# Silu straight from the front's sums, quad 3's input split by columns, and a new order of all steps in a one-core scan kernel

## The chip, the cores and the metric

The kernel runs on one core of a Trainium2 chip, as one launch. The metric is the device time of one execution in microseconds (us), median of several. A core has five engines with queues of their own: PE (matmul), DVE (vector), ACT (activations and copies), POOL (elementwise here) and SP, whose queue only starts DMAs. Each engine runs its own instructions in the order in which they are written; between engines there are only semaphores. SBUF is the working memory, PSUM the eight banks of 128 partitions x 512 f32 that PE writes. POOL here reads and writes SBUF only.

## The reference, cut to what matters

The input is (8, 96, 64, 64) f32, seen as 8 batches of 4096 tokens with 96 channels. Layer 0 is a group norm, a selective-scan block with layer norm, and a residual. Layer 1 is an attention that is linear (no softmax), folded into one 97 x 97 matrix per batch, and a feed-forward part with rounding to 8-bit floats.

```python
xz = u @ in_proj_w.T                                   # 96 -> 2 x 192
xm, z = xz[..., :192], xz[..., 192:]
xm = silu(causal_conv4(xm) + conv_b)                   # the "u" of the kernel
dt, Bm, Cm = split(xm @ x_proj_w.T, [6, 22])           # 6, 16 and 16 columns
delta = softplus(dt @ dt_proj_w.T + dt_proj_b)
h = exp(delta * A) * h + delta * Bm * xm               # per channel and state: 192 x 16 chains of 4096
y = (sum over states of h * Cm + xm * D) * silu(z)
x = x + layernorm(y @ out_proj_w.T)
t = t + linear_attention(layernorm(t)); t = t + quantized_ffn(layernorm(t))
```

## The kernel before, in words

**Tiles.** The tokens are cut into 64 chunks of T = 512 (8 to a batch). The 192 x 16 recurrences of a chunk fill 24 tiles of 128 partitions x 512, in 6 quads of 4: quads 0 to 3 hold channels 0 to 127, quads 4 and 5 the other 64. For every tile (quad `s`, place `q`) there are a decay on ACT (`decay`, L837: DA = exp(A x delta), into one of two PSUM banks), a scan on DVE (`scan`, L1210: R = DA x R + D along time) and, for each quad, a product with C on POOL (`product`, L663), which PE sums over states into bank Y (`sum_states`, L1523 and L1527). As there are two DA banks, decay j waits for scan j-2, and scan j waits for decay j.

**The inputs D.** D = (delta x u) x B is made quad by quad into three buffers (quad s uses buffer s mod 3). Quads 0 and 1 are made by DVE (L1192), which reads B from a PSUM bank PB that ACT fills just before (`put_b`, L823). Quads 2, 4 and 5 are made by POOL (L642). Of quad 3 DVE makes tiles 0 and 1 (128 x 1024, L1192) and POOL tiles 2 and 3 (128 x 1024, `rest`, L651). The first writer of a buffer waits until the quad that held it is scanned: `rest` and DVE's part of quad 3 wait for quad 0, POOL's quad 4 for quad 1, quad 5 for quad 2.

**The front** (of chunk g+2 in iteration g) is PE's: the convolution over four taps in two parts (512 columns for channels 0 to 127, L1480; 256 for the others, L1483) and the two parts of z (L1446). ACT copies these four sums from PSUM into `raw` in SBUF (`front_evac`, L776 and L780), three of them in iteration g and the last in g+1, and in iteration g+1 takes Silu of `raw` into u and z, 128 x 768 each (`silu`, L786 and L792). Silu and Exp/Ln are in different tables, so a table load of 1283 ns stands before and behind each such pair. Then follow the projection of u (L1498, L1500), its evacuation `state_rows` (L800), `dt_proj`, `parts` (L809), `softplus` (L813), `delta` on DVE (L1220) and delta x u on POOL (`du`, L635). SP writes delta, du and B/C rows to DRAM and reads them back spread over partitions (`ds`, `us`, `Bs`, `Cs`).

**The order** is written out by hand, one function `iteration(g)` for each engine: steps of chunk g (scans), of g+1 and g+2 (front), of g-1 and g-2 (out projection, layer norm, tokens) and of g-10 to g-12 (feed-forward: `norm_x2` L1296, `result` L1301, `up`, `hidden`, `down`). The chunks g-10 and later exist only from iteration 10 on. The two additions of the change's title are `add_x` (L1241, residual of layer 0) and `result` (L1301, residual of the feed-forward), both on DVE.

**PSUM.** Banks G0 to G3 pass from one short use to the next within an iteration. PE waits for the last reader of a bank by calls `freed(progress, k, n)` ahead of the new writer.

Of the kernel before, what the change touches and what calls it, by code (L numbers as in the profile page):

```python
# [9 lines left out]
T = 512  # L10
CH = L // T
HALO = TAPS - 1
S = T + 1
LOW = 128
# [29 lines left out]

BY_DVE = {0: 1, 1: 2, 3: 3}
BY_POOL = {2: 1, 3: 2, 4: 3, 5: 4}
OURS = {3: 2}
# [10 lines left out]
def build(nc, I, cols, out):  # L58
# [7 lines left out]
    with ctx:  # L66
# [135 lines left out]
        raw = sb("raw", [LOW, 2, W2])  # L202
# [69 lines left out]
        front_ev = Progress("front_ev", 4)  # L272
        silued = Progress("silued", 2)
# [24 lines left out]
        by_act = [normed, gset, gn_mean, gn_dev, gn_act, front_ev, silued, st_done, sp_done, b_put, exp_done, post_act,  # L298
# [316 lines left out]
        def _(pool):  # L615
            credit(nc.gpsimd, by_pool)

            def first_delta_u():

                pool.wait_ge(dl_low, 1)  # L620
                pool.wait_ge(silued.sem, silued.at(0, 1))
# [4 lines left out]
            def delta_u(k):  # L626
# [5 lines left out]
                pool.wait_ge(silued.sem, silued.at(k, 1))  # L632
# [12 lines left out]
            def rest(k, s):  # L645
                n = OURS[s]
# [4 lines left out]
                nc.gpsimd.tensor_tensor(D[:, s % NDBU, n:QUAD, :], us[:, n:QUAD, :],  # L651
                                        Bs[:, h, w, :].unsqueeze(1).to_broadcast([128, QUAD - n, T]),
# [43 lines left out]
        def _(act):  # L696
# [70 lines left out]
            def front_evac(k, n, src):  # L767
                evac(k, n, src, n + 1)

            def evac(k, n, src, after):  # L770
                act.wait_ge(front_mm.sem, front_mm.at(k, after))
                if n == 0:
                    act.wait_ge(silued.sem, silued.at(k - 1, 1 if k == 1 else None))
                if n in (0, 3):
                    v = n // 3
                    nc.scalar.activation(raw[:, 0, part(v)], src[:, 0:T - H * v], ACT.Identity,  # L776
                                         bias=cb[:, v:v + 1]).then_inc(front_ev.sem, 1)
                else:
                    v = n - 1
                    nc.scalar.copy(raw[:, 1, part(v)], src[:, 0:T - H * v]).then_inc(front_ev.sem, 1)  # L780
# [1196 lines left out]
```

## Time and profile before

| | us |
|---|---|
| median of 3 runs (2616.61 to 2617.24) | 2617.11 |
| the profiled execution | 2615.23 |
| its span, first to last instruction | 2613.3 |
| DVE busy (97% of the span) | 2538.6 |
| POOL busy (92%) | 2411.7 |
| ACT busy (91%) | 2379.0 |
| PE busy (82%) | 2132.9 |

The granted TensorE clock is 0.934 of full speed on average. Busy time of an instruction runs from its start to its end, and neighbours on one engine overlap a little, so what one more instruction costs its engine is the distance between starts where they stand back to back; the timeline shows it.

### The profile page before, as it was taken

The page shows a single profiled execution, that of the slowest core. Times are in us where ns is not written, and L with a number is a line of the kernel's source. Part 1 is how long each engine was busy: PE and PEld are TensorE (multiplying, and loading weights), DVE is VectorE, ACT ScalarE, POOL GpSimd, SP SyncE. Part 2 cuts the span into 40 slices and gives each one's busy share as a digit, 9 for nine tenths or more (in the row PEclk, how much of TensorE's full clock was granted, in tenths as well). Part 3 has the DMA queues.
Part 4 walks back from the last instruction along what each step waited for, and adds up shares of the span by engine and source line. Part 5 has one row for each costly group of instructions (what it writes and reads, how often), then busy time and mean ns, then how long its engine had stood idle before and what let it go on. Part 6 is the DMA issues. An engine that isn't in the chain of part 4 may idle for free.

```text
span 2613.3 us, 34371 instructions
## 1 busy us (share of the span) xinstructions
PE 2132.9 (82%) x9844; PEld 774.2 (30%) x9844; DVE 2538.6 (97%) x2503; ACT 2379.0 (91%) x3971; POOL 2411.7 (92%) x718
## 2 busy tenths in 40 slices
PE   6677777888888888888888888888888888888878
PEld 3222223323323323323323323323323323323323
DVE  6999999999999999999999999999999999999996
ACT  5777778999999999999999999999999999999977
POOL 4999999999999999999999999999999999999981
PEclk8888888899999999999999999999999999999979
DMA  6455555655656656555656565565566565556533
GB/s 249 165 188 165 175 178 168 201 190 189 212 190 192 207 191 203 195 196 194 199 200 197 192 202 196 192 203 195 191 207 199 184 202 192 186 197 200 171 124 88
DMA packets 171161, 494.43 MB, mean 189 GB/s; under 512 B 23040, under 2 KB 44672, under 8 KB 154144
## 3 DMA queue, kind: packets, MB, share of 16 engines
q1 hardware_dynamic: 170976, 492.25, 56.8%
q8 instruction: 81, 1.33, 0.2%
q14 instruction: 104, 0.85, 0.1%
HBM read 400.28 MB, written 91.88 MB: 188 GB/s over the span
## 4 chain that ended last, share of the span: by engine, by line
DVE 48%; issue 23%; ACT 16%; POOL 8%; PE 4%; DMA 1%; SPq 0%; DVEq 0%; ACTq 0%; POOLq 0%
DVE R L1210 32%; DVE D L1192 8%; ACT DA L837 5%; POOL R L663 3%; POOL D L642 3%; DVE yv L1231 2%; ACT dl L809 2%; DVE xq L1241 1%; ACT un L764 1%; ACT rs L848 1%; ACT PB L823 1%; DVE th L1249 1%; DVE xt L1301 1%; DVE q L1296 1%; ACT fsq L886 1%
## 5 line engine op out<-in xcount | busy, mean ns | idle before, releaser
L1210 DVE TENSOR_TENSOR_SCAN R<-DA,R,D 128x512 f32<-128x512 f32 x1344 | 1642.4, 1265 | 21.4 <-ACT DA L837 19.9
L663 POOL TENSOR_TENSOR R<-R,Cs 128x2048 f32<-128x2048 f32 x383 | 1456.0, 3817 | 103.8 <-DVE R L1210 103.3
L837 ACT ACTIVATE DA<-ds,kept_w 128x512 f32<-128x512 f32 x1536 | 1044.3, 686 | 158.3 <-DVE R L1210 145.5
L642 POOL TENSOR_TENSOR D<-us,Bs 128x2048 f32<-128x2048 f32 x193 | 736.7, 3817 | 8.5 <-DMA us<-lo_d 8.1
L1192 DVE TENSOR_TENSOR D<-us,PB 128x2048 f32<-128x2048 f32 x191 | 363.2, 1901 | 5.7 <-ACT PB L823 5.7
L1523 PE MATMUL Y<-R,kept_w 128*32 128x512 f32 x2048 | 289.6, 659 | 9.0 <-POOL R L663 8.9
L1480 PE MATMUL G<-un,wcv 96*128 96x512 f32 x512 | 261.5, 658 | 20.6 <-ACT rs L848 10.6
L1210 DVE TENSOR_TENSOR_SCAN R<-DA,D 128x512 f32<-128x512 f32 x192 | 222.4, 1204 | 8.7 <-ACT DA L837 8.7
L1446 PE MATMUL G<-sq,kept_w 96*96 96x512 f32 (+1 forms) x256 | 145.5, 651 | 78.0 <-ACT h L900 46.7
L1527 PE MATMUL Y<-R,kept_w 128*32 128x256 f32 x2048 | 158.3, 434 | 5.5 <-POOL R L663 5.5
L1446 PE MATMUL G<-st,kept_w 128*64 128x256 f32 (+1 forms) x384 | 112.5, 485 | 57.4 <-ACT st L800 57.4
L1480 PEld LDWEIGHTS G<-un,wcv 96*128 96x128 f32 x512 | 100.9, 207 | 181.1 <-issue 111.6
L1446 PE MATMUL G<-q,w1q 96*128 96x512 fp8e5 x164 | 67.1, 410 | 105.3 <-ACT rs L848 74.1
L1483 PE MATMUL G<-un,wcv 96*64 96x256 f32 x1024 | 149.4, 416 | 0.0
L651 POOL TENSOR_TENSOR D<-us,Bs 128x1024 f32<-128x1024 f32 x64 | 128.0, 2000 | 0.0
L1537 PE MATMUL Y<-u,kept_w 64*64 64x256 f32 x256 | 49.6, 470 | 91.0 <-DVE yv L1231 90.9
L904 ACT ACTIVATE h<-h,b1q 128x512 f16<-128x512 f16 x165 | 112.0, 711 | 0.0
L1446 PE MATMUL G<-un,kept_w 96*128 96x512 f32 x372 | 110.3, 485 | 0.2
L823 ACT COPY PB<-Bs 128x512 f32<-128x512 f32 x191 | 110.2, 577 | 0.0
L1523 PEld LDWEIGHTS Y<-R,kept_w 128*32 128x32 f32 x2048 | 48.9, 117 | 192.9 <-issue 124.6
L1483 PEld LDWEIGHTS G<-un,wcv 96*64 96x64 f32 x1024 | 65.0, 141 | 128.9 <-issue 110.1
L1498 PE MATMUL G<-u,kept_w 128*128 128x512 f32 x128 | 71.7, 642 | 36.7 <-ACT u L786 36.7
(224 smaller groups left out, 3323.5 us busy)
## 6 DMA issues: line engine op xcount, KB each, us to landing
Bs<-bc_d SPq DMA_DIRECT2D x128, 512.0 KB, 5.2
us<-lo_d SPq DMA_DIRECT2D x64, 1024.0 KB, 6.6
ds<-lo_d SPq DMA_DIRECT2D x64, 1024.0 KB, 6.5
Cs<-bc_d SPq DMA_DIRECT2D x128, 512.0 KB, 4.8
us<-hi_d SPq DMA_DIRECT2D x64, 512.0 KB, 7.2
ds<-hi_d SPq DMA_DIRECT2D x64, 512.0 KB, 4.6
lo_d<-dl SPq DMA_DIRECT2D x64, 256.0 KB, 2.0
lo_d<-du SPq DMA_DIRECT2D x64, 256.0 KB, 2.0
```

The source lines that it names most:

```text
L642: nc.gpsimd.tensor_tensor(shaped(D[:, s % NDBU, :, :], s), low(us, s) if s in LOWS else high(us), of_states(Bs, s), ALU.mult).then_inc(don ...
L651: nc.gpsimd.tensor_tensor(D[:, s % NDBU, n:QUAD, :], us[:, n:QUAD, :], Bs[:, h, w, :].unsqueeze(1).to_broadcast([128, QUAD - n, T]), ALU.m ...
L663: nc.gpsimd.tensor_tensor(shaped(R[:, s, :, 0:T], s), shaped(R[:, s, :, 1:S], s), of_states(Cs, s), ALU.mult).then_inc(hc_done.sem, 1)
L823: nc.scalar.copy(PB[:, :], Bs[:, h, w, :]).then_inc(b_put.sem, steps_to(k, s))
L837: nc.scalar.activation(DA[j % NDA][:, :], ds[:, i, :], ACT.Exp, scale=A[:, j:j + 1]).then_inc(exp_done.sem, 1)
L1192: nc.vector.tensor_tensor(D[:, s % NDBU, 0:n, :], us[:, 0:n, :], PB[:, :].unsqueeze(1).to_broadcast([128, n, T]), ALU.mult)\
L1210: nc.vector.tensor_tensor_scan(R[:, s, q, 1:S], DA[j % NDA][:, :], D[:, s % NDBU, q, :], before, ALU.mult, ALU.add).then_inc(scanned.sem, 1)
L1446: return mm(o, left, right, start=True, stop=True)
L1480: last = mm(o[:, :], wcv[:, t, 0:LOW], un[:, t:t + T], start=(t == 0), stop=(t == TAPS - 1))
L1483: last = mm(o[rows, 0:H], wcv[:, t, LOW:LOW + HIGH], un[:, t + cs.start:t + cs.stop], start=(t == 0), stop=(t == TAPS - 1))
L1523: last = mm(Y[32 * q:32 * q + 32, :], sumsel, R[:, s, q, 0:T], start=s == 0, stop=s == 3)
L1527: last = mm(Y[at:at + 32, 0:H], sumsel, R[:, s, q, cs], start=False, stop=s == 5 and q > 1)
```

## The change

1. **Silu reads PSUM.** `raw` and the four copies into it are gone. `silu(k, *src)` takes u's two parts and z's two parts from the banks G3, G1 (columns 0 to 255), G2, G1 (columns 256 to 511): four activations instead of two, with the bias inside. So G1, G2 and G3 stay taken from the end of iteration g to the middle of g+1, and the waits on `front_ev` become waits on `silued`, which counts four.
2. **Quad 3 is shared by columns.** DVE makes columns 0 to 127 of all four tiles (4 x 128), POOL columns 128 to 511 (4 x 384). `put_b` copies 128 columns for it. The scan of quad 3's first tile now waits for both.
3. **All of `iteration(g)` is reordered** on ACT, DVE, PE and POOL; SP's queue keeps its order.
4. Both additions stay on DVE, with the same operands' shapes.

```diff
-OURS = {3: 2}
+FRONT = (3, 1, 4, 2)
+SPLIT = {3: 128}
...
 def rest(k, s):
-    n = OURS[s]
+    cs = slice(SPLIT[s], T)
...
-    nc.gpsimd.tensor_tensor(D[:, s % NDBU, n:QUAD, :], us[:, n:QUAD, :],
-                            Bs[:, h, w, :].unsqueeze(1).to_broadcast([128, QUAD - n, T]),
+    nc.gpsimd.tensor_tensor(D[:, s % NDBU, :, cs], us[:, 0:QUAD, cs],
+                            Bs[:, h, w, cs].unsqueeze(1).to_broadcast([128, QUAD, T - SPLIT[s]]),
                             ALU.mult).then_inc(dbu_p.sem, 1)
...
-            def silu_u(k, after=None):
-                act.wait_ge(front_ev.sem, front_ev.at(k, after))
+            def silu(k, *src):
                 act.wait_ge(skipped.sem, skipped.at(k - 2))
                 act.wait_ge(du_done.sem, du_done.at(k - 2))
-                nc.scalar.activation(u[:, place(k) % 2, :], raw[:, 0, :], ACT.Silu).then_inc(silued.sem, 1)
+                for v in range(2):
+                    act.wait_ge(front_mm.sem, front_mm.at(k, FRONT[v]))
+                    nc.scalar.activation(u[:, place(k) % 2, part(v)], src[v], ACT.Silu, bias=cb[:, v:v + 1])\
+                        .then_inc(silued.sem, 1)
                 if there(k - ZS):
                     act.wait_ge(gated.sem, gated.at(k - ZS))
-                nc.scalar.activation(z[:, k % ZS, :], raw[:, 1, :], ACT.Silu).then_inc(silued.sem, 1)
+                for v in range(2):
+                    act.wait_ge(front_mm.sem, front_mm.at(k, FRONT[2 + v]))
+                    nc.scalar.activation(z[:, k % ZS, part(v)], src[2 + v], ACT.Silu).then_inc(silued.sem, 1)
                 nc.scalar.preload_act_table_set(EXP_LN)
...
-                nc.scalar.copy(PB[:, :], Bs[:, h, w, :]).then_inc(b_put.sem, steps_to(k, s))
+                n = SPLIT.get(s, T)
+                nc.scalar.copy(PB[:, 0:n], Bs[:, h, w, 0:n]).then_inc(b_put.sem, steps_to(k, s))
...
-                n = OURS.get(s, QUAD)
-                nc.vector.tensor_tensor(D[:, s % NDBU, 0:n, :], us[:, 0:n, :],
-                                        PB[:, :].unsqueeze(1).to_broadcast([128, n, T]), ALU.mult)\
+                n = SPLIT.get(s, T)
+                nc.vector.tensor_tensor(D[:, s % NDBU, :, 0:n], us[:, 0:QUAD, 0:n],
+                                        PB[:, 0:n].unsqueeze(1).to_broadcast([128, QUAD, n]), ALU.mult)\
...
             def iteration(g):            # POOL
                     inputs(g, 2)
+                    rest(g, 3)
                     product(g, 0)
-                    rest(g, 3)
                     inputs(g, 4)
...
             def iteration(g):            # DVE, its end
                     scan(g, 5, 1)
+                    scan(g, 5, 2)
+                    scan(g, 5, 3)
...
                 if there(g + 1):
                     inputs(g + 1, 0)
-                if there(g):
-                    scan(g, 5, 2)
...
-                    scan(g, 5, 3)
```

**POOL, one iteration from the last product of the chunk before.** L663 is a product, L642 a whole input, L651 the shared input of quad 3, L635 delta x u. Before:

```order
L663 TENSOR_TENSOR R<-R,Cs 128x4x512 [waits c_in1,scanned]
L642 TENSOR_TENSOR D<-us,Bs 128x4x512 [waits u_in0,b_in1,scanned]
L663 TENSOR_TENSOR R<-R,Cs 128x4x512 [waits c_in0,scanned]
L651 TENSOR_TENSOR D<-us,Bs 128x2x512 [waits u_in0,b_in1,scanned]
L642 TENSOR_TENSOR D<-us,Bs 128x4x512 [waits u_in1,b_in0,scanned]
L635 TENSOR_TENSOR du<-dl,u 128x768 [waits du_out,silued,dl_done]
```

The same stretch of the changed program:

```order
L663 TENSOR_TENSOR R<-R,Cs 128x4x512 [waits c_in1,scanned]
L642 TENSOR_TENSOR D<-us,Bs 128x4x512 [waits u_in0,b_in1,scanned]
L651 TENSOR_TENSOR D<-us,Bs 128x4x384 [waits u_in0,b_in1,scanned]
L663 TENSOR_TENSOR R<-R,Cs 128x4x512 [waits c_in0,scanned]
L642 TENSOR_TENSOR D<-us,Bs 128x4x512 [waits u_in1,b_in0,scanned]
L635 TENSOR_TENSOR du<-dl,u 128x768 [waits du_out,silued,dl_done]
```

Quad 3's input is half as large again and stands ahead of quad 0's product; the rest of POOL's iteration is as it was.

**DVE, from the second tile of quad 5 to the fourth tile of quad 0** of the next chunk. The rows with `R<-DA` are scans, the row `D<-us,PB` before a `yv` or between scans is an input, `yv` the gate, `th` the token norm. Before:

```order
L1210 SCALAR_TENSOR_TENSOR R<-DA,R,D 128x512 [waits exp_done]
L1192 TENSOR_TENSOR D<-us,PB 128x4x512 [waits u_in0,b_put,scanned]
L1210 SCALAR_TENSOR_TENSOR R<-DA,R,D 128x512 [waits exp_done] x2
L1231 TENSOR_TENSOR yv<-Y,z 128x512 [waits post_mm,summed]
L1210 SCALAR_TENSOR_TENSOR R<-DA,R,D 128x512 [waits summed,dbu_d,exp_done]
L1210 SCALAR_TENSOR_TENSOR R<-DA,R,D 128x512 [waits exp_done]
L1249 TENSOR_TENSOR th<-G,rs 96x512 [waits th_out,post_mm,post_act]
L1210 SCALAR_TENSOR_TENSOR R<-DA,R,D 128x512 [waits exp_done]
L1192 TENSOR_TENSOR D<-us,PB 128x4x512 [waits u_in0,b_put,scanned]
L1210 SCALAR_TENSOR_TENSOR R<-DA,R,D 128x512 [waits exp_done]
```

The changed program:

```order
L1180 SCALAR_TENSOR_TENSOR R<-DA,R,D 128x512 [waits exp_done] x3
L1256 COPY gp<-G 96x192 [waits fold_mm]
L1164 TENSOR_TENSOR D<-us,PB 128x4x512 [waits u_in0,b_put,scanned]
L1201 TENSOR_TENSOR yv<-Y,z 128x512 [waits post_mm,summed]
L1180 SCALAR_TENSOR_TENSOR R<-DA,R,D 128x512 [waits summed,dbu_d,exp_done]
L1180 SCALAR_TENSOR_TENSOR R<-DA,R,D 128x512 [waits exp_done]
L1219 TENSOR_TENSOR th<-G,rs 96x512 [waits th_out,post_mm,post_act]
L1180 SCALAR_TENSOR_TENSOR R<-DA,R,D 128x512 [waits exp_done] x2
L1164 TENSOR_TENSOR D<-us,PB 128x4x512 [waits u_in0,b_put,scanned]
```

The next chunk's first input stands behind all scans of quad 5 instead of between them, and quad 1's input behind all four scans of quad 0. (The copy `gp` is there once in eight chunks.)

**ACT, the stretch around the Silus.** `DA<-ds` rows are decays, `PB<-Bs` is `put_b`, `rs` the standard deviation, `st` is `state_rows`, `tT` the token copy. Before:

```order
L823 COPY PB<-Bs 128x512 [waits dbu_d,b_in0]
L837 ACTIVATE DA1<-ds,kept_w 128x512 [waits scanned]
L776 ACTIVATE raw<-G1,kept_w 128x256 [waits front_mm]
L852 ACTIVATE rs<-rs 96x512 [waits post_ln]
L837 ACTIVATE DA0<-ds,kept_w 128x512 [waits scanned]
L837 ACTIVATE DA1<-ds,kept_w 128x512 [waits scanned]
L786 ACT_TABLE_LOAD [waits du_done,skipped]
L786 ACTIVATE u<-raw 128x768 [waits front_ev]
L792 ACTIVATE z<-raw 128x768 [waits gated]
L793 ACT_TABLE_LOAD
L837 ACTIVATE DA0<-ds,kept_w 128x512 [waits scanned,d_in0]
L837 ACTIVATE DA1<-ds,kept_w 128x512 [waits scanned]
```

The changed program, from the third decay of quad 0:

```order
L825 ACTIVATE DA1<-ds,kept_w 128x512 [waits scanned]
L773 ACT_TABLE_LOAD [waits front_mm,du_done]
L773 ACTIVATE u<-G3,kept_w 128x512 [waits skipped]
L773 ACTIVATE u<-G1,kept_w 128x256 [waits front_mm]
L779 ACTIVATE z<-G2 128x512 [waits front_mm,gated]
L779 ACTIVATE z<-G1 128x256 [waits front_mm]
L780 ACT_TABLE_LOAD
L825 ACTIVATE DA0<-ds,kept_w 128x512 [waits scanned,d_in0]
L787 ACTIVATE st<-G3,kept_w 128x512 [waits bc_out,back_mm]
L825 ACTIVATE DA1<-ds,kept_w 128x512 [waits scanned]
L868 COPY tT<-G2 128x4x96 [waits post_mm]
```

The pair of Silus is four, its table load waits for the front's matmuls, and `state_rows` now stands ahead of quad 1's second decay instead of behind it.

## Rows read from the trace of the kernel before

**Rows 1.** The profile's page: span, and each engine's busy time.
```profile
span 2613.3 us, 34371 instructions
PE 2132.9 (82%) x9844; PEld 774.2 (30%) x9844; DVE 2538.6 (97%) x2503; ACT 2379.0 (91%) x3971; POOL 2411.7 (92%) x718
```

**Rows 2.** Busy time by stretch: PE, PEld, DVE, ACT, POOL, then PEclk, DMA share, GB/s.
```profile
87.00:400.00 313.00, 229.32 (x1075) 82.95 (x1074) 297.40 (x275) 234.57 (x379) 295.50 (x87) 0.85 0.52 174
1339.00:1652.00 313.00, 260.88 (x1230) 93.84 (x1230) 311.62 (x302) 303.01 (x515) 300.30 (x89) 0.97 0.59 197
```

**Rows 3.** Waits in 87 to 400 us: total us, times, longest.
```profile
ACT raw L776 <- PE G L1480: 18.9, 8, 3.1
DVE R L1210 <- ACT DA L837: 15.6, 23, 2.1
```

**Rows 4.** POOL timeline around 2000 us: start, length, operation, [idle before, releaser].
```profile
2003.00 3.82 POOL L663 TENSOR_TENSOR R<-R,Cs 128x2048 f32<-128x2048 f32 x1 [0.77 <-DVE R L1210]
2006.78 1.99 POOL L651 TENSOR_TENSOR D<-us,Bs 128x1024 f32<-128x1024 f32 x1
2008.74 3.81 POOL L642 TENSOR_TENSOR D<-us,Bs 128x2048 f32<-128x2048 f32 x1
2012.51 1.54 POOL L635 TENSOR_TENSOR du<-dl,u 128x768 f32<-128x768 f32 x1
2014.01 3.81 POOL L663 TENSOR_TENSOR R<-R,Cs 128x2048 f32<-128x2048 f32 x1
...
2033.90 3.81 POOL L663 TENSOR_TENSOR R<-R,Cs 128x2048 f32<-128x2048 f32 x1 [0.99 <-DVE R L1210]
```

**Rows 5.** DVE timeline, the same stretch.
```profile
1999.20 2.26 DVE L1192 TENSOR_TENSOR D<-us,PB 128x2048 f32<-128x2048 f32 x1
2001.38 0.35 DVE L1290 COPY MT<-G 97x192 f32<-97x192 f32 x1
...
2002.84 0.66 DVE L1301 TENSOR_TENSOR xt<-G,y 96x512 f32<-96x512 f32 x1
2003.42 0.41 DVE L1231 TENSOR_TENSOR yv<-Y,z 128x256 f32<-128x256 f32 x1
...
2013.09 1.20 DVE L1192 TENSOR_TENSOR D<-us,PB 128x1024 f32<-128x1024 f32 x1
2014.20 1.28 DVE L1210 TENSOR_TENSOR_SCAN R<-DA,R,D 128x512 f32<-128x512 f32 x1
2015.39 0.73 DVE L1235 SCALAR_TENSOR_TENSOR G<-G,kept_w,rs 96x512 f32<-96x512 f32 x1
```

**Rows 6.** SP timeline: the first load of B for the next chunk; its landing.
```profile
2015.64 0.56 SPq L510 DMA_DIRECT2D Bs<-bc_d x1
DMA to landing us min/median/max: 3.8/3.8/3.8
```

**Rows 7.** Start of the program: Silu read from PSUM, both widths.
```profile
17.19 0.69 ACT L1084 ACTIVATE u<-G,kept_w 128x512 f32<-128x512 f32 x1 [2.43 <-PE G L1480]
19.00 0.47 ACT L1084 ACTIVATE u<-G,kept_w 128x256 f32<-128x256 f32 x1 [1.12 <-PE G L1483]
```

**Rows 8.** ACT timeline, later: the Silus and their table loads.
```profile
2037.58 1.28 ACT L786 ACT_TABLE_LOAD   x1
2038.87 0.84 ACT L786 ACTIVATE u<-raw 128x768 f32<-128x768 f32 x1
2041.76 0.69 ACT L837 ACTIVATE DA<-ds,kept_w 128x512 f32<-128x512 f32 x1
```

**Rows 9.** POOL's delta x u alone, 91 to 409 us: window, busy (x count).
```profile
91.00:409.00 318.00, 12.40 (x8) 0.86 0.52 174
```

**Rows 10.** PE timeline: a convolution behind idle time, and one without (iteration 50).
```profile
211.47 1.10 PE L1446 MATMUL G<-sq,kept_w 96*96 96x512 f32 x2 [2.70 <-DVE dl L1220]
213.34 5.40 PE L1480 MATMUL G<-un,wcv 96*128 96x512 f32 x8 [0.77 <-ACT rs L848]
2014.33 3.70 PE L1480 MATMUL G<-un,wcv 96*128 96x512 f32 x8
```

More of the change, by code:

```diff
@@ L967, in iteration @@
                 if there(g):
+                    decay(g, 2, 2)
                     put_b(g, 3)
+                if there(g + 2):
+                    norm(g + 2)
+                if there(g):
                     decay(g, 2, 3)
@@ L971, in iteration @@
                     square_x2(g - 10, G2)
-                if there(g + 2):
-                    norm(g + 2)
                 if there(g - 1):
@@ L976, in iteration @@
                     inv_std(g - 1, 0)
-                if place(g + 3) == 0 and later(g + 3):
-                    group_scale(g + 3, PB, 2)
-                if inside(g - 11):
-                    output_bias(g - 11)
                 if there(g):
@@ L1303, in iteration @@
             def iteration(g):
-                if place(g + 3) == 0 and later(g + 3):
-                    aggregate(g + 3)
                 if there(g - 1):
@@ L1314, in iteration @@
                     scan(g, 0, 2)
-                    inputs(g, 1)
-                if place(g - 10) == 0 and early(g - 10):
-                    fold(g - 10, 4, G1)
+                if place(g + 3) == 0 and later(g + 3):
+                    aggregate(g + 3)
                 if there(g):
                     scan(g, 0, 3)
+                    inputs(g, 1)
                 if inside(g - 12):
-                    result(g - 12, G2)
+                    result(g - 12, G0)
                 if there(g - 1):
@@ L1327, in iteration @@
                     scan(g, 1, 2)
+                if place(g - 10) == 0 and early(g - 10):
+                    fold(g - 10, 4, G1)
+                if there(g):
                     scan(g, 1, 3)
-                    scan(g, 2, 0)
                 if there(g - 2):
@@ L1332, in iteration @@
                 if there(g):
+                    scan(g, 2, 0)
                     scan(g, 2, 1)
                 if there(g + 1):
-                    delta(g + 1, G3, G0)
+                    delta(g + 1, *((G3, G0) if g < 0 else (G0, G3)))
                 if there(g):
                     scan(g, 2, 2)
+                if place(g - 9) == 0 and early(g - 9):
+                    fold(g - 9, 1, G0)
+                if there(g):
+                    scan(g, 2, 3)
                     inputs(g, 3)
-                    scan(g, 2, 3)
                 if there(g - 1):
@@ L1343, in iteration @@
                     scan(g, 3, 0)
+                if place(g - 9) == 0 and early(g - 9):
+                    fold(g - 9, 2, G3)
                 if there(g - 1):
@@ L1704, in iteration @@
                 if place(g + 3) == 0 and later(g + 3):
                     group_var(g + 3, PB)
+                if there(g - 2):
+                    (freed(post_act, g - 2, 5) or freed(silued, g + 1, 3))
+                    gram(g - 2, G2)
+                if there(g + 1):
+                    freed(st_done, g + 1)
+                    dt_proj(g + 1, 1, G3)
+                if place(g - 10) == 0 and early(g - 10):
+                    (freed(f_y16, g - 11) or freed(silued, g + 1))
+                    fold(g - 10, 4, G1)
@@ new lines, in iteration @@
+                if there(g + 2):
+                    (freed(post_dve, g - 1, 2) or (place(g - 10) == 0 and freed(fold_ev, g - 10, 4))
+                     or freed(f_y16, g - 11) or freed(silued, g + 1))
+                    conv(g + 2, 1, G1, (0, 1))
+                if there(g - 1):
+                    (freed(f_h16, g - 10, 1) or freed(f_q8, g - 10) or freed(post_dve, g - 2)
+                     or freed(post_act, g - 2, 5) or freed(silued, g + 1, 3))
+                    variance(g - 1, 1, G2)
```

300 lines of the change are left out of this document (124 added, 176 removed).

## The prediction

> **What bounds the kernel now.** I read the page first: DVE is busy for 97% of the span [rows 1]. The rest could lie in a few holes, so the busy time by stretch comes next. Batch by batch (8 chunks, 313 us in the middle of the program) DVE is busy for 311.6 of 313.0 us and POOL for 300.3 [rows 2]. From 400 to 2500 us the period is therefore 313.0 / 8 = 39.1 us per chunk and is DVE's own work: about 0.17 us per chunk is idle. The first batch, 87 to 400 us, is different: DVE is busy for only 297.4 us [rows 2], since the feed-forward steps begin at iteration 10, and yet it lasts as long. There scans wait 15.6 us in 23 pieces for decays, and ACT itself waits 18.9 us for the convolution before its copy into raw [rows 3]. So two things can shorten the program: less work on DVE in the long middle, and fewer late decays in the first batch.
>
> The engine in second place matters as much. What an instruction costs its engine is the distance between starts of neighbours. On POOL a 2048-wide one takes 3.77 us (2008.74 to 2012.51), the 1024-wide one 1.96, delta x u 1.50 [rows 4]. A chunk has nine of the first kind: 9 x 3.77 + 1.96 + 1.50 = 37.4 us of 39.1, and the missing 1.7 are its two waits for DVE's scans, 0.77 and 0.99 [rows 4].
>
> **Quad 3's input, DVE's part.** It is 1024 elements now and 512 after. A 2048-wide input costs 2.18 us on DVE, a 1024-wide one 1.11 [rows 5], so 1.045 ns per element; 512 come to 1.11 - 0.535 = 0.58 us, which is also the distance at a single 512-wide operation (2002.84 to 2003.42) [rows 5]. Gain: 0.535 us per chunk. The bounds are 0.53 and, if four rows of 128 cost more than one of 512, 0.3 (a 256-wide operation still takes 0.41 [rows 5], against 0.66 at 512, so 0.25 per 256); I take 0.535.
>
> **POOL's part.** 1024 become 1536. (3.77 - 1.96) / 1024 = 1.77 ns per element, so 1.96 + 0.91 = 2.87 us, and the chunk's sum is 38.3 us. Bounds: 2.8, and 3.77 if only the instruction counted. DVE's sum falls to about 39.1 - 0.17 - 0.535 = 38.4. POOL has 0.1 us left per chunk: it is all but a second bound, and any wait on it becomes time unless DVE has slack at that spot.
>
> A rule speaks against this move. The Trainium skill, GPSIMD Engine Reference, in its table of which engine suits an operation, prefers VectorE for elementwise work on two inputs and puts GpSimd at about twice the time. The rows say 1.77 against 1.045 ns per element, 1.7 times, so the trace agrees in direction. By two times 1.045 the added part of POOL would be 1.07 us instead of 0.91, and its sum 38.5, above DVE's 38.4.
>
> **POOL's waits in the new order.** I set t = 0 at the end of quad 5's last scan and add up starts: an input 2.18, a scan 1.19 (2014.20 to 2015.39), a 512-wide operation 0.58, gate 2 0.33, delta 0.91 [rows 5]. DVE then ends quad 0 at 8.1, quad 1 at 16.0, has delta done at 19.4, ends quad 2 at 21.8, quad 3 at 29.1, quad 4 at 33.8 and quad 5 at 38.4. POOL's new order: the input of quad 4 waits for quad 1 and starts at 16.1. From there: 19.9 (delta is there), delta x u to 21.4, product 1 to 25.1, input 5 to 28.9, products 2, 3, 4 to 40.3, product 5 to 44.0, input 2 to 47.8, the shared input to 50.7, product 0 to 54.4, and the next input of quad 4 may start at 54.5. No other wait binds. Product 4 ends 1.9 us behind quad 5's last scan, where before POOL sat waiting 0.99 for that scan [rows 4]. Who reads POOL: the first gate needs PE's sum of quad 3, whose product ends at 36.5, and is due at 40.6; quad 3's scan is due at 23, its POOL part is done at 12; quads 4 and 5 have 9 and 5 us.
>
> **What hangs on delta x u.** It ends at 21.4. Before it ended at 2014.05, and SP issued the load of B at 2015.64, landing 3.8 us later [rows 6], so 5.4 us behind. Now B lands at 26.8, and ACT's copy to PB, which moved ahead of quad 4's first decay, is due at 26.8 to 27.3. That decay ends near 28.1, and its scan is due at 29.0. Cover: 0.9 us.
>
> **ACT.** Removed are four reads of PSUM of the widths that take 0.69 and 0.47 in [rows 7], so up to 2.3 us less 0.1 overlap each, 1.9 us per chunk, and 384 of 512 columns of one copy to PB. Added: Silu from PSUM takes 0.69 and 0.47 [rows 7], twice each, 2.3 us less four overlaps, against two of 0.84 less two [rows 8]: 0.3 to 0.4 us more between the table loads. Net some -1.5 us and the PB columns on an engine that is busy 303 of 313 [rows 2]. In the middle this is worth nothing by itself, since DVE waits for ACT almost never there. But the path through the Silus is tight: from the first table load to quad 1's first decay it is 4.18 us now [rows 8] and 4.5 after. With quad 0's last decay in front (0.62) and quad 1's first behind (0.69) and some 0.1 for the semaphore that is 5.9 us, against DVE's work from the end of quad 0's second scan to quad 1's first: token norm 0.58, two scans 2.38, quad 1's input 2.18, `result` 0.58, gate 2 0.33, together 6.05. Cover 0.15 us. I followed the rest of ACT's queue in the same way; the next tight places are quad 2's last decay (cover 0.2) and the standard deviation before scale_out (0.2). Each could leak. I put 0.1 us per chunk for them.
>
> **PE.** u's projection reads G3 and is released by Silu at t = 8.3; PE is then still in the feed-forward sum (6.5 to 8.5), so it ends at 10.5, and `state_rows`, now ahead of quad 1's second decay, runs at 10.9. That decay ends at 12.1, its scan is due at 12.4. The front's sums are done by t = 2 to 3 of the next iteration, the Silus ask at 5.9. Holding three banks costs nothing by this count.
>
> **The first batch.** The ACT copies that waited for the convolution are gone from between quad 3's and 4's decays, so most of the 15.6 us [rows 3] go too. Without the feed-forward steps DVE needs about 297.4 / 8 - 0.5 = 36.7 us per chunk, so POOL bounds these chunks at 38.3. From 91 to 409 us POOL does delta x u eight times [rows 9], so the period there is 39.75 us. I take 38.5 after, POOL's sum and a little: -1.25 x 8 = -10 us. Bounds: -11.6 (POOL's sum alone) and 0 (other waits take their place).
>
> **Start and end.** The first decay waits for the DMA of delta, not for Silu, and the tail behind the last scan is PE's queue. I take 0, within 2 us.
>
> **Sum.** Middle: 54 chunks x 0.535 = -28.9. First batch -10. Leaks 54 x 0.1 = +5.4. Together -33.5. On the profiled execution, 2615.2 us (1.9 above its span [rows 1] and 1.9 below the median), that is 2581.7; on the median, 2617.1 - 33.5 = 2583.6, and since the leaks are a guess on the high side I say 2583.
>
> **Rivals.** A. Decays leak (chance 0.17). ACT's covers of 0.15 to 0.3 us are smaller than what I add up by eye. If scans wait 0.3 us more per chunk, 54 x 0.3 = 16 us come back: 2599. For it: `state_rows` and the standard deviation stand ahead of decays. Against it: ACT has over 1.5 us less to do, and 1.4 us idle on DVE per batch [rows 2] shows how well such covers hold.
>
> B. POOL becomes the bound (0.12). If its shared input costs 3.3 instead of 2.87, or a wait appears in its queue, the period is 38.8 to 39.0: the middle gains only 0.1 to 0.3 us per chunk, 54 x 0.2 = 11 us, with the first batch at -8: 2617 - 19 = 2598.
>
> C. PE falls to the lower clock in front of u's projection (0.06), slower than before. A convolution behind 2.70 us of idle time took 5.40 us, where another took 3.70 [rows 10]; the granted clock is 0.85 of full in the first batch and 0.97 in a later one [rows 2], a mean over 1.2 and 2.4 GHz. At half clock the projection takes 4 us instead of 2, `state_rows` comes 2 us late, quad 1's second decay and scan with it, less 0.3 cover: +1.7 us per chunk, 64 x 1.7 = 109, less the 33: about 2693. It decides where the projection is later than the cover, 0.3, and the gain per chunk, 33 / 64 = 0.5, together: from 0.8 us on. Against it: in the new order PE has the sums of quads 4 and 5 and a feed-forward sum to do until the projection, with gaps of under 1.5 us. The Trainium skill, TensorE: Matmul & The Clock Gate, on the clock gate, has the same two speeds after idle and busy time; the 5.40 against 3.70 agree.
>
> D. Nothing is gained (0.03): the 0.5 us on DVE return as waits on decays everywhere, 2610 to 2620.
>
> **Numbers.** The forecast has 0.62 (own range 2572 to 2592). The range for 8 in 10 reaches from 2570, where no leak and the first batch's -11.6 come together (2617.1 - 28.9 - 11.6 = 2576.6), with 6 us for what is idle now and may go as well, to 2604, which takes in A and B. Faster by more than 0.2% (5.2 us, about what the measurement can tell from no change): 0.91 from the forecast, A and B, less some of D; within: 0.03; slower: 0.06.
>
> **What would show it.** Right: DVE's input of quad 3 at about 0.66 us long, 4 x 128; POOL's at 2.9 us; batches in the middle 308.5 to 310 us apart; DVE idle there at most 3 us per batch; POOL's only regular wait before quad 4's input, under 0.3 us; delta x u 38.3 to 38.9 us apart in the first nine chunks; no idle time before PE's projection above 1 us. Wrong: `DVE R <- ACT DA` as a total above 25 us in the middle (A), DVE waiting for POOL's D or PE's Y, or POOL above 98% busy with a period over 38.7 (B), u's projection at 1.2 us per part (C).

## The result and the profile after

The changed kernel takes 2621.0 us (median of 18 runs, 2616.0 to 2625.1) beside 2616.1 for the kernel before on the same chip (18 runs): a ratio of 1.0017, interval [1.0010, 1.0024]. Not 34 us less, but no gain at all. The page of the changed kernel, its span and busy times, to be read against [rows 1]:

```profile
span 2614.2 us, 34179 instructions
PE 2237.3 (86%) x9844; PEld 803.7 (31%) x9844; DVE 2507.5 (96%) x2503; ACT 2269.2 (87%) x3845; POOL 2467.1 (94%) x718
```

The work moved as planned. DVE has 31 us less than before, ACT 110 less, POOL 55 more. But TensorE, whose instructions are as many as before (9844), is busy 104 us longer: its matmuls got slower. The same two stretches as in [rows 2] (PE, PEld, DVE, ACT, POOL, then PEclk, DMA share, GB/s) say where:

```profile
87.00:400.00 313.00, 242.36 (x1113) 85.28 (x1112) 304.23 (x287) 230.98 (x380) 312.28 (x90) 0.84 0.53 177
1339.00:1652.00 313.00, 277.00 (x1228) 98.90 (x1227) 306.56 (x302) 288.46 (x496) 305.98 (x89) 0.88 0.60 196
```

In the first batch POOL is now busy for 312.3 of 313 us, the bound that the prediction named, and by the starts of delta x u in the POOL timeline the chunks are 38.3 to 38.6 us apart: 8.3 us are gained up to the tenth. In the middle eight chunks take 314.0 us by the same starts, where the prediction had 308.5 to 310 and the kernel before 312.5 to 312.8 (the 313.0 of the prediction is the width of its window). DVE is idle there for 6.4 us, against 1.4, and the granted clock of TensorE is 0.88, against 0.97. What DVE waits for in 1339 to 1653 us (total, times, longest):

```profile
DVE yv L1201 <- PE Y L1492: 3.3, 4, 1.1
DVE gp L1256 <- PE G L1415: 2.6, 1, 2.6
```

Those are the first gate, waiting for TensorE's sum of quad 3, and the copy of a fold's result, once per batch. Together they are 5.9 us; the batch is 4.0 to 5.5 us longer than forecast. No scan waits for a decay there any more. One of the gate's waits, in TensorE's timeline of the changed kernel (start, length, operation, [idle before, releaser]):

```profile
1543.65 1.02 PE L1503 MATMUL Y<-u,kept_w 128*128 128x512 f32 x2
1546.62 1.07 PE L1415 MATMUL G<-xq,kept_w 96*96 96x512 f32 x2 [1.94 <-DVE xq L1211]
1548.39 0.59 PE L1415 MATMUL G<-q,w1q 96*128 96x512 fp8e5 x2 [0.70 <-DVE q L1266]
1548.91 1.97 PE L1452 MATMUL G<-un,wcv 96*64 96x256 f32 x8
1551.99 1.99 PE L1415 MATMUL G<-sq,kept_w 96*96 96x512 f32 x2 [1.11 <-ACT sq L831]
1553.91 1.98 PE L1452 MATMUL G<-un,wcv 96*64 96x256 f32 x8
1555.82 1.94 PE L1492 MATMUL Y<-R,kept_w 128*32 128x512 f32 x8
...
1559.24 1.07 PE L1492 MATMUL Y<-R,kept_w 128*32 128x512 f32 x8
1560.23 1.98 PE L1449 MATMUL G<-un,wcv 96*128 96x512 f32 x4
1562.15 1.07 PE L1492 MATMUL Y<-R,kept_w 128*32 128x512 f32 x8
```

Read it from above: the matmuls on `xq` are the step `centre`, those on `sq` the variance, those on `q` the feed-forward's `up`, L1452 and L1449 the two parts of the convolution, L1492 the sum of a quad. Behind `add_skip` (L1503) TensorE stands for 1.94 us until DVE has made `xq`, then 0.70, then 1.11. From 1548.91 on its instructions take twice their time: half a convolution of 8 small matmuls 1.97 us (1.08 elsewhere), the sum of quad 1 1.94, where quad 2's and 3's take 1.07. The last row is the sum of quad 3. POOL's product for it is done near 1557.8 (the third behind 1546.48, 3.8 us each), TensorE comes to the sum at 1562.15, and the gate that needs it is due at 1562.19, when DVE's input of 1559.93 (below) ends. The windows show the granted clock itself:

```profile
1550.00:1555.00 5.00, 3.89 (x14) 0.50 1.00 403
1555.00:1560.00 5.00, 5.00 (x27) 0.59 0.56 224
1560.00:1565.00 5.00, 5.00 (x21) 1.00 0.36 104
```

A share of 0.50 is the lower of the two levels, 1.2 GHz. And DVE, on its timeline, at the same time:

```profile
1559.93 2.26 DVE L1164 TENSOR_TENSOR D<-us,PB 128x2048 f32<-128x2048 f32 x1
1563.28 0.69 DVE L1201 TENSOR_TENSOR yv<-Y,z 128x512 f32<-128x512 f32 x1 [1.09 <-PE Y L1492]
```

The gate stands ahead of quad 0's scans, so they all slide by 1.09 us and POOL waits for them in turn. This is no single case: of the eight chunks in this stretch seven have a granted clock of 0.61 over the 13 us from `xq`'s matmul on and one 0.87, and four of the eight gates wait. The idle time in front of `xq`'s matmul is 1.86 to 2.35 us in the eight chunks, 16.6 us in all. In the kernel before, the same place holds the first part of the convolution, 3.70 us of matmuls at 2014.33 [rows 10]; its bank was free early, since ACT had copied it to `raw`. Around it, in before's timeline of TensorE, nothing stands still, and the granted clock in 2008 to 2022 is 1.00:

```profile
2013.14 1.07 PE L1446 MATMUL G<-fsq,kept_w 96*96 96x512 f32 x2
...
2017.96 1.07 PE L1523 MATMUL Y<-R,kept_w 128*32 128x512 f32 x8
...
2019.92 1.02 PE L1446 MATMUL G<-xq,kept_w 96*96 96x512 f32 x2
```

`xq` (the last row) is long there when TensorE comes to it. In the changed kernel the convolution's bank has to keep its result for Silu, the convolution stands behind quad 2's sum, and the gap is empty.

Where the time went, by the starts of delta x u in both profiled executions (spans 2613.3 and 2614.2 us):

| stretch | forecast | measured |
|---|---|---|
| up to the tenth start (410.1 and 401.7 us) | -10 | -8.3 |
| from there to the last, 53 chunks (2071.8 and 2081.4 us) | -23.5 | +9.6 |
| behind the last | 0 | -0.3 |

So 33 of the 34.5 us by which the sum missed lie in the middle.

The durations came out as worked out: DVE's part of quad 3's input (DVE timeline) and POOL's (POOL timeline):

```profile
1582.82 0.65 DVE L1164 TENSOR_TENSOR D<-us,PB 128x512 f32<-128x512 f32 x1
1569.36 2.90 POOL L651 TENSOR_TENSOR D<-us,Bs 128x1536 f32<-128x1536 f32 x1 [0.21 <-DVE R L1180]
```

### The profile page after: what moved, and what is told of

Its sections match the earlier page's. It is cut to its first block and busy times, and to the rows that moved or that the text cites. A ratio compares the mean times of both kernels' runs of the same rounds, so it can differ in the third digit from the quotient of the medians.

```text
span 2614.2 us, 34179 instructions
## 1 busy us (share of the span) xinstructions
PE 2237.3 (86%) x9844; PEld 803.7 (31%) x9844; DVE 2507.5 (96%) x2503; ACT 2269.2 (87%) x3845; POOL 2467.1 (94%) x718
## 5 line engine op out<-in xcount | busy, mean ns | idle before, releaser
L663 POOL TENSOR_TENSOR R<-R,Cs 128x2048 f32<-128x2048 f32 x383 | 1453.3, 3817 | 0.0
L642 POOL TENSOR_TENSOR D<-us,Bs 128x2048 f32<-128x2048 f32 x193 | 736.7, 3817 | 45.1 <-DVE R L1180 36.2
L1492 PE MATMUL Y<-R,kept_w 128*32 128x512 f32 x2048 | 325.4, 714 | 17.9 <-POOL R L663 17.9
L1164 DVE TENSOR_TENSOR D<-us,PB 128x2048 f32<-128x2048 f32 x191 | 328.8, 1722 | 5.3 <-DMA us<-lo_d 5.3
L1415 PE MATMUL G<-sq,kept_w 96*96 96x512 f32 (+1 forms) x256 | 191.2, 839 | 95.5 <-ACT sq L831 68.0
L1449 PE MATMUL G<-un,wcv 96*128 96x512 f32 x512 | 255.8, 623 | 0.1
L1452 PE MATMUL G<-un,wcv 96*64 96x256 f32 x1024 | 240.0, 620 | 0.0
L1415 PE MATMUL G<-xq,kept_w 96*96 96x512 f32 x128 | 92.1, 811 | 142.5 <-DVE xq L1211 142.5
L651 POOL TENSOR_TENSOR D<-us,Bs 128x1536 f32<-128x1536 f32 x64 | 186.3, 2911 | 11.8 <-DVE R L1180 11.2
L1452 PEld LDWEIGHTS G<-un,wcv 96*64 96x64 f32 x1024 | 94.3, 206 | 179.0 <-issue 176.5
L1449 PEld LDWEIGHTS G<-un,wcv 96*128 96x128 f32 x512 | 87.6, 190 | 171.2 <-issue 127.5
L1415 PE MATMUL G<-un,kept_w 96*64 96x256 f32 x372 | 117.6, 548 | 0.0
L888 ACT CAST h<-G 128x512 f16<-128x512 f32 x164 | 95.1, 580 | 24.8 <-PE G L1415 24.1
L1415 PEld LDWEIGHTS G<-sq,kept_w 96*96 96x96 f32 x256 | 40.4, 206 | 190.3 <-issue 117.0
L635 POOL TENSOR_TENSOR du<-dl,u 128x768 f32<-128x768 f32 x63 | 97.5, 1548 | 0.0
```

What stands on the lines that cost most here:

```text
L642: nc.gpsimd.tensor_tensor(shaped(D[:, s % NDBU, :, :], s), low(us, s) if s in LOWS else high(us), of_states(Bs, s), ALU.mult).then_inc(don ...
L651: nc.gpsimd.tensor_tensor(D[:, s % NDBU, :, cs], us[:, 0:QUAD, cs], Bs[:, h, w, cs].unsqueeze(1).to_broadcast([128, QUAD, T - SPLIT[s]]), ...
L663: nc.gpsimd.tensor_tensor(shaped(R[:, s, :, 0:T], s), shaped(R[:, s, :, 1:S], s), of_states(Cs, s), ALU.mult).then_inc(hc_done.sem, 1)
L1164: nc.vector.tensor_tensor(D[:, s % NDBU, :, 0:n], us[:, 0:QUAD, 0:n], PB[:, 0:n].unsqueeze(1).to_broadcast([128, QUAD, n]), ALU.mult)\
L1415: return mm(o, left, right, start=True, stop=True)
L1449: last = mm(o[:, :], wcv[:, t, 0:LOW], un[:, t:t + T], start=(t == 0), stop=(t == TAPS - 1))
```

## The experiments

The theory from here on: TensorE's idle time behind `add_skip` is followed by matmuls at half clock, these make quad 3's sum late, and that takes the gain. The first rival: the order of the steps makes the sum late whatever the clock. "Batch" below is the distance of eight starts of delta x u in the middle (before 312.6, after 314.0 us). Each ratio is to the kernel before, measured beside it on the same chip; the times of different experiments come from three chips, on which the kernel before took 2613.9 to 2616.0 us, so their differences are good to about 2 us.

### 1. One gap filled

```diff
                 if there(g):
                     add_skip(g, 0)
+                if inside(g - 10):
+                    (freed(post_ln, g - 1, 1) or freed(dl_done, g + 1))
+                    spin(4, G3, *weights)
```

`spin` is the kernel's own helper: matmuls of 256 columns whose result is overwritten. `spin(4, ...)` is eight instructions, 1.89 us. They run from the iteration on in which the feed-forward steps begin.

> The changed kernel with four more matmuls in each iteration (dummy ones, 128x256, into bank G3 while it is free, behind add_skip and ahead of the wait for add_x); nothing else differs. Theory 'PE idles, then runs at half clock': the idle stretch of 1.9 us before centre is filled, so the convolutions and sums behind it run at full clock (half a convolution of the second part 1.1 us instead of 2.0), the first gate no longer waits for the sum of quad 3 and the fold's copy waits less. The period in the middle falls from 39.25 to 38.5 to 38.8 us, the run to 2585 to 2600, although PE has 2 us more to do per chunk. Rival 'PE has too much to do in the new order' or 'POOL is the bound': more matmuls cannot help; the time stays at 2621 or grows by up to 2 us per chunk, 2640 and more.

Measured: 2615.1 us, ratio 0.9999 [0.9989, 1.0008], batch 312.9 to 314.1: at most 6 us less than the changed kernel. Hardly anything. But TensorE's timeline showed a second gap:

```profile
1466.71 1.07 PE L1415 MATMUL G<-xq,kept_w 96*96 96x512 f32 x2 [0.38 <-DVE xq L1211]
1468.48 0.59 PE L1415 MATMUL G<-q,w1q 96*128 96x512 fp8e5 x2 [0.70 <-DVE q L1266]
1469.00 1.08 PE L1452 MATMUL G<-un,wcv 96*64 96x256 f32 x8
1472.08 1.44 PE L1415 MATMUL G<-sq,kept_w 96*96 96x512 f32 x2 [2.00 <-ACT sq L831]
1473.46 1.98 PE L1452 MATMUL G<-un,wcv 96*64 96x256 f32 x8
```

The filling closed the first gap (0.38 us left) and the next matmuls ran at full speed, so TensorE reached the variance sooner and waited 2.00 us there for ACT; half clock came behind this gap instead, in six of the eight chunks of the middle stretch. The expectation failed in its time; the row explains why one filling is no test of the cause.

### 2. The split alone, in the kernel before

```diff
-OURS = {3: 2}
+SPLIT = {3: 128}
```

with the input, `rest` and `put_b` as in the change; the order and `raw` stay.

> The kernel before with the column split of quad 3's input alone (DVE 4x128, POOL 4x384, 128 columns of PB); raw, its copies and the old order stay. Theory: the split is worth its DVE time, 0.53 us per chunk in the middle and nothing in the first batch, where late decays bound: 2617 - 25 = 2590 (2586 to 2598), if POOL's waits of 1.7 us per chunk take its added 0.9. Rival 'the split itself costs, POOL becomes the bound': 2610 to 2625.

Measured: 2600.4 us, ratio 0.9945 [0.9929, 0.9962], batch 310.1 to 310.3, 2 us outside the slow end of the range. Here the convolution still stands in the gap and the granted clock of the middle is 0.96. The chunk of the middle is 0.32 us shorter (2055.1 against 2071.8 us for 53), not 0.53: scans now wait for decays 2.8 us in 9 pieces there, against 1.1 before, and the first batch is hardly shortened (409.0 against 410.1 us to the tenth start). So the rest of the change (order and Silu from PSUM), as it stands, costs about 20 us, more than the split brings here.

### 3. Half the convolution back into the gap, the rest early

Against after; hidden 1 then goes through G2 and behind `decay(5, 1)`:

```diff
+                    conv(g + 2, 0, G3, (0, 1))        # behind add_skip, ahead of centre
...
                     up(g - 10, 0, G2)
-                    up(g - 10, 1, G3)
+                if there(g + 2):
+                    conv(g + 2, 0, G3, (2, 3))
```

> The changed kernel with real work in PE's gap instead of dummies: the front's first convolution (G3) starts right behind add_skip, half of it ahead of centre and half behind up 0; the second hidden part goes through G2 instead of G3 (up 1 and its copy later). Theory 'idle, then half clock': the PE queue behind the gap runs at full clock and is 4 us shorter ahead of quad 3's sum; the gate waits vanish, 2585 to 2600. Rival 'POOL is the bound': at most 5 us faster than the changed kernel. A risk of this edit alone: the copies of hidden 1 and 2 come within 3 us on ACT and delay the last decays by some tenths, up to +10 us.

Measured: 2599.3 us, ratio 0.9940 [0.9925, 0.9954], batch 310.6. No gate waits for TensorE any more. The edit moves hidden 1 as well, so by itself it does not show that the gap was the cause; it does show that G3 could hold the convolution from `add_skip` on. What remains sits elsewhere: TensorE now stands still ahead of the second `add_skip`, for 3.02 us in front of this row (which then takes 1.12 us, against 0.65 at 1556.66), and DVE waits 2.0 us for decays and 1.0 for `result`.

```profile
1402.21 1.12 PE L1505 MATMUL Y<-u,kept_w 64*64 64x256 f32 x4 [3.02 <-DVE yv L1200]
```

### 4. The fold's copy later

```diff
-                if place(g - 9) == 0 and early(g - 9):
-                    fold(g - 9, 3, G2)
                 if there(g + 1):
                     inputs(g + 1, 0)
+                if place(g - 9) == 0 and early(g - 9):
+                    fold(g - 9, 3, G2)
```

> The changed kernel with one pair of steps swapped on DVE: the fold's third copy (once per 8 chunks, it waited 2.6 us for PE) behind the next chunk's first input instead of ahead of it. If each term of the loss stands by itself, 2.2 us of the 2.6 go, seven times: -13 to -16 us, 2606. If DVE's waits there are only slack that POOL or the gate wait takes over, 0 to -5 us.

Measured: 2613.9 us, ratio 0.9992 [0.9983, 1.0001], 7 us less than the changed kernel and between the two forecasts, but the batch is 314.0 as before the edit. The wait of 2.6 us shrank to 0.5, and the gates' grew:

```profile
DVE yv L1201 <- PE Y L1492: 5.6, 6, 1.5
DVE gp L1256 <- PE G L1415: 0.5, 1, 0.5
```

The sum stayed at 6 us. The two waits are not two costs but one, TensorE being late; taking away one place where it shows only moves it.

### 5. The order alone, without the split

After, with `OURS = {3: 2}` and the quad shared as before.

> The kernel after, with quad 3's input shared by quads again (DVE two quarters of four, POOL the other two): the new order and Silu from PSUM alone, without the split by columns. Theory (TensorE's late sum of quad 3 sets the time of a chunk of the middle batches, and the split's saving disappears in the wait behind it): putting back the longer DVE work (+0.53 us per chunk) fills the waits of the gates, so the batch stays near 314 to 315 and the time is 2615 to 2625, the first batch back at 40 us per chunk (about +10). Rival (the two edits add up: the split is worth 16 us, the new order costs 20): the batch of eight chunks is 317 to 318 and the time 2634 to 2640.

Measured: 2684.9 us, ratio 1.0268 [1.0253, 1.0283], batch 324.3. Both expectations failed: within this order the split is worth 64 us, four times what it brings alone. The gates wait for TensorE longer, 7.8 us in the stretch against 3.3. TensorE's timeline:

```profile
1379.95 1.99 PE L1414 MATMUL G<-xq,kept_w 96*96 96x512 f32 x2 [2.48 <-DVE xq L1210]
...
1382.73 1.98 PE L1451 MATMUL G<-un,wcv 96*64 96x256 f32 x8
1385.33 1.99 PE L1414 MATMUL G<-sq,kept_w 96*96 96x512 f32 x2 [0.62 <-ACT sq L830]
```

DVE's input of quad 3 is queued ahead of `xq`. With 1.19 us instead of 0.66 it lengthens the first gap: 2.48 us here, 18.6 us in the eight chunks of the stretch against 16.6 in after. The matmul right behind the gap runs at half clock in five of the eight chunks, in after wholly in two. That the change's two parts are joined by that gap is so far an argument; experiment 8 tests it.

### 6. Two taps in the gap, two left late

As 3, but taps 2 and 3 of the convolution stay behind quad 3's sum.

> The kernel after with taps 0 and 1 of the front's first convolution in TensorE's gap between add_skip and centre, taps 2 and 3 left behind quad 3's sum, up 1 and hidden 1 through the bank G2 late. Theory (work in that gap keeps the clock, work behind quad 3's sum keeps it before the next chunk's add_skip): no wait of gp and yv for TensorE in the middle batches over 0.3 us, batch 310 to 311, time 2596 to 2602; against the version that moves all four taps the gap of 3 us in front of add_skip (g-1, 1) is 2 us shorter and the decays' wait of 0.4 to 0.7 us once per chunk is gone if that gap caused it. Rival (the taps early do not keep the clock because only half of the gap is filled): the waits of 0.8 to 1.1 us remain in some chunks, batch 312 to 313, time 2606 to 2614.

Measured: 2704.3 us, ratio 1.0344 [1.0329, 1.0359], batch 327.7: the worst of all, beyond the rival too. The second gap (2.05 us) is back, and behind it the half clock:

```profile
1392.37 1.08 PE L1451 MATMUL G<-un,wcv 96*64 96x256 f32 x8
1395.50 2.00 PE L1414 MATMUL G<-sq,kept_w 96*96 96x512 f32 x2 [2.05 <-ACT sq L831]
1397.43 1.98 PE L1451 MATMUL G<-un,wcv 96*64 96x256 f32 x8
```

`up` 1 stands behind these rows, in the order of experiment 3: ACT waits for the ups 22.2 us in 1339 to 1653 us, its decays are held up behind that, and DVE waits 19.7 for them. What of this is the clock and what the later hidden steps was not taken apart.

### 7. Both gaps filled

Experiment 1 and four such matmul pairs more:

```diff
                 if there(g + 2):
                     (freed(post_dve, g - 1, 2) or ... or freed(silued, g + 1))
+                    if inside(g - 10):
+                        spin(4, G1, *weights)
                     conv(g + 2, 1, G1, (0, 1))
```

> The kernel after with four idle matmul pairs of 256 columns (results overwritten) into G3 in front of centre and four more into G1 in front of the second convolution, from the tenth chunk on: both of TensorE's gaps of about 2 us are filled, no order is changed. Theory (idle time lowers TensorE's clock, and the matmuls at half clock make quad 3's sum and the first gate late): granted clock over 0.95 in 1339 to 1652, the waits of yv and gp for TensorE from 3.3 and 2.6 us to under 1 in a middle batch, batch 310.5 to 312, time 2598 to 2606. Rival (the order of the steps alone makes the sum late, the clock is a bystander): the waits stay at 2.5 us and more though the clock is over 0.95, batch 313 to 314, time 2613 to 2620.

Measured: 2580.8 us, ratio 0.9870 [0.9853, 0.9886], batches of 308.2 to 310.2: below even the range of the theory, and far from the rival's. Its page, its middle stretch and the same place in TensorE's timeline:

```profile
span 2580.1 us, 35823 instructions
PE 2241.7 (87%) x10692; PEld 919.8 (36%) x10692; DVE 2504.6 (97%) x2503; ACT 2265.7 (88%) x3845; POOL 2465.2 (96%) x718
```

```profile
1339.00:1652.00 313.00, 282.13 (x1376) 117.71 (x1376) 310.11 (x305) 291.46 (x504) 310.14 (x90) 0.99 0.60 200
```

```profile
1486.39 1.89 PE L1415 MATMUL G<-kept_w 128*128 128x256 f32 x8
1488.49 1.07 PE L1415 MATMUL G<-xq,kept_w 96*96 96x512 f32 x2 [0.21 <-DVE xq L1211]
...
1490.69 1.89 PE L1415 MATMUL G<-kept_w 128*128 128x256 f32 x8
1492.52 1.08 PE L1452 MATMUL G<-un,wcv 96*64 96x256 f32 x8
...
1495.88 1.07 PE L1492 MATMUL Y<-R,kept_w 128*32 128x512 f32 x8
```

With 848 more matmuls in the trace than after, TensorE is busy only 4 us longer; its clock is 0.99, neither gate waits for it, and the time is 40 us less (38 by the two ratios). No step changed its place and TensorE only got more to do, so it is through the clock that the order makes the sum late. This version beats both kernels.

### 8. Both gaps filled, without the split

> The version with both of TensorE's gaps filled (2580.8 us), with quad 3's input shared by quads again. Theory (the gaps' half clock joined the two parts of the change: with both gaps filled they are apart, and the split is worth its own duration on DVE): 54 chunks of 0.53 us, 29 us, and about 10 us in the first batch where DVE sets the time again, so 2606 to 2622, batch of eight chunks 312 to 314, and no waits of the gates for TensorE above 1 us in 313. Rival (the split is worth the 64 us that it brought between the version with the order alone, 2684.9, and the kernel after, 2621.0, whatever the clock does): 2640 to 2648, batch 317 and more.

Measured: 2616.2 us, ratio 1.0001 [0.9992, 1.0010], batches of 313.2 to 313.9. Its middle stretch, with a clock of 1.00:

```profile
1339.00:1652.00 313.00, 279.04 (x1358) 116.11 (x1358) 311.34 (x301) 291.81 (x498) 299.33 (x88) 1.00 0.59 197
```

The theory's numbers: with the gaps filled the split is worth 35 us (2616.2 - 2580.8) and not 64. By the starts of delta x u 3.8 of them lie ahead of the tenth (405.6 against 401.8 us), 28.3 in the 53 chunks behind it, where the prediction's term for the split is 28.9, and 3.9 behind the last. And without the split the filled new order takes the time of the kernel before, where unfilled it took 69 us more (experiment 5): what the order costs is the clock.

### 9. Only the second gap filled

> The kernel after with the four filling matmul pairs only in front of the second convolution (G1), the gap in front of centre left idle. Theory (each gap by itself is followed by a stretch at half clock, and a sum of quad 3 late by one of them already takes the gain): the matmuls behind centre at half clock in some chunks, waits of yv and gp between 1 and 5 us in 313, batch 312 to 314, time 2604 to 2618. Rival (only the second gap, the one nearest to quad 3's sum, matters): waits under 1 us, batch 309 to 310, time 2578 to 2586.

Measured: 2589.9 us, ratio 0.9897 [0.9882, 0.9911], batches of 310.2 to 310.7: between the ranges of the theory and the rival. One filling in front of the second convolution gives 31 of the 40 us, the other alone 6. The first gap is as long as in after (16.6 us in eight chunks). In two of the eight everything behind it runs at full clock. In the other six half clock does come, but it falls for the most part on the filling matmuls, which nobody waits for, and the sums run at full clock. One chunk of each kind:

```profile
1530.77 1.07 PE L1415 MATMUL G<-xq,kept_w 96*96 96x512 f32 x2 [1.94 <-DVE xq L1211]
1532.97 1.89 PE L1415 MATMUL G<-kept_w 128*128 128x256 f32 x8
...
1538.16 1.07 PE L1492 MATMUL Y<-R,kept_w 128*32 128x512 f32 x8
```

```profile
1491.57 1.10 PE L1415 MATMUL G<-xq,kept_w 96*96 96x512 f32 x2 [1.94 <-DVE xq L1211]
...
1494.15 3.62 PE L1415 MATMUL G<-kept_w 128*128 128x256 f32 x8
...
1501.53 1.07 PE L1492 MATMUL Y<-R,kept_w 128*32 128x512 f32 x8
```

So two gaps of equal length, 1.94 us, have half clock behind them once and once not, and what half clock costs depends on what stands there: here idle matmuls, in after convolutions and sums. The filling also keeps the second gap short (0.27 us in the chunk of 1530.77, 1.11 in after's of 1546.62). The theory's waits did not come back: no gate waits for TensorE, only `gp`, 1.2 us.

### 10. A control: the same matmuls elsewhere

```diff
+                    if inside(g - 10):
+                        spin(4, G2, *weights)
                     z_proj(g + 2, 0, G2)
```

> A control: the kernel after with four filling matmul pairs in front of z's first projection, which is behind quad 3's sum and in neither gap. Theory (only the two gaps count): granted clock of the middle batch near 0.88, waits of yv and gp for TensorE as in after (5 to 7 us in 313), time 2616 to 2632. Rival (more TensorE work anywhere keeps the clock up): clock above 0.95, batch under 311, time below 2600.

Measured: 2699.0 us, ratio 1.0310 [1.0293, 1.0327], batch 327.7, clock 0.87. The same work on TensorE does nothing for its clock at this place, outside the gaps; that part of the theory held. The time did not: 70 us above what I expected. Behind quad 3's sum TensorE has no room: u's projection and what follows it come later, so `st` on ACT waits for it 9.9 us in the middle, decays are late behind `st`, and the first gate waits as in after. ACT's and DVE's waits in 1339 to 1653 us:

```profile
ACT st L787 <- PE G L1469: 9.9, 7, 1.6
DVE yv L1201 <- PE Y L1492: 5.5, 7, 1.4
DVE R L1180 <- ACT DA L825: 5.1, 7, 0.8
DVE xt L1271 <- PE G L1613: 3.6, 6, 0.6
```

## Why the prediction was wrong

**The step that failed** is the prediction's sentence on TensorE: "Holding three banks costs nothing by this count." The count held the banks against the times at which Silu and the front's sums are due, and in after's middle ACT waits for none of the front's matmuls. It did not ask what the banks had allowed: in the kernel before the convolution fills the time in which TensorE would otherwise wait for `add_x` [rows 10]. Moving it behind quad 2's sum leaves 1.9 us idle there and 1.1 ahead of the variance, and half clock behind them. Measured price: 5.9 us of DVE's waits per batch and 31.5 us over the 53 chunks of the middle (2081.4 against 2049.9); removed by experiment 7 without any change of order. It is not the bank alone that keeps the convolution out of the gap: experiment 3 starts it there in the same G3, with `up` 1 sent through another bank.

**The first gate.** In "who reads POOL" I gave the first gate from 36.5, the end of quad 3's product, to 40.6, as if TensorE were there the moment POOL was done. POOL kept its part: its product was done near 1557.8, 2.1 us ahead of the end of quad 5's last scan (t = 36.3). In the trace the sum starts at 1562.15 with no wait for POOL in front of it, right behind half a convolution, 4.4 us behind POOL. A cover has to be counted on every engine that the operand passes through.

**Rival C had the mechanism and the wrong place.** It looked for idle time in front of u's projection, found gaps under 1.5 us and got 0.06. There it was right (in after's middle ACT waits for that projection nowhere). The same question was not put to the stretch behind `add_skip`, though [rows 10] showed a wait for `dl` of 2.70 us and a slow convolution behind it. The Trainium skill, TensorE: Matmul & The Clock Gate, in its part on HAM oscillation, describes a matmul loop that waits for a DMA once in each pass, 3 to 5 us long, and starts each pass at the slow clock. The traces agree in kind, 0.88 granted over the middle batch of after and 0.99 with the gaps filled, but with waits that are shorter: none of TensorE's for `xq` in that stretch is over 2.4 us.

**What came out.** DVE's input 0.65 to 0.66 us; POOL's 2.90 (2.87 forecast). The first batch, bounded by POOL at 38.3 us: 8.3 us gained, where 10 was said. The scans' waits for decays there fell from 15.6 us [rows 3] to 5.3, in the middle to nothing; so the leaks of rival A did not come, and B's wait (the gate for Y) came by another cause. And the sum itself: with TensorE's clock kept up the version of experiment 7 takes 2580.8 us, 2 us from the forecast 2583, and its middle chunks are 0.41 us shorter than those of before (2049.9 against 2071.8 us for the 53 chunks from the tenth start on), where 0.535 - 0.1 = 0.435 was said. Most of its chunks are 38.3 to 38.6 us apart, POOL's bound and a little, with one longer one, 39.3 to 41.1, in each batch. That the total comes so near is in part luck: 2.9 us are gained behind the last start, where the prediction had nothing, and stand in for what the middle and the first batch lack. And the agreement is that of another kernel than the one forecast; it shows that the terms were sized well, not that the forecast held.

**What stays open.** Whether before's own 3% below full clock is worth anything; why gaps of the same length are followed by half clock in one chunk and not in another; what of experiments 6 and 10 (chunks of 41.0 us each) is clock and what is delay of the hidden steps and of u's projection; and whether useful work could fill both gaps as well as idle matmuls do. Experiment 3 used the convolution for it and ended 18 us short of experiment 7.

## What to carry to other kernels

When a change moves TensorE's work, list what the moved piece had stood in front of and behind, and read the idle time that it leaves, not only whether TensorE still has time: behind two waits of a microsecond or two the matmuls took twice as long, and that took a gain of 34 us on engines that never got busier. Compare TensorE's busy time at an equal count of instructions (9844 in both) first; here 104 us more busy time for the same instructions was the clock. Where nothing useful fits into the gap, a few matmuls whose result nobody reads are worth a try, placed in the gap itself: the same four pairs were worth -31 us in one place and +78 in another (not all of the latter is the clock, see experiment 10).

## What the runs showed of the hardware that was not expected

- The half clock's price is far from proportional to the idle time. The first gap grew by 0.25 us on average, from 2.08 to 2.33 (16.6 and 18.6 us in eight, experiment 5), and the chunk from 39.25 to 40.5 us, of which 0.53 is DVE's longer input.
- Filling one gap can open the next: TensorE at full speed arrives sooner and waits for the variance's operand 14.9 us in eight chunks where it had waited 8.1 (experiment 1; 2.00 against 1.11 in the chunks shown).
- Matmuls put into a gap help even where half clock comes all the same: in experiment 9 it fell on them in most chunks (3.62 us for the eight, against 1.89), and the sums behind them ran at full clock.
- Two fillings, 848 more matmuls in the trace, raised TensorE's busy time by only 4.4 us (2237.3 to 2241.7), since the others ran faster.
